# First layer's bank with the router runs three tiles ahead of the other two; turn to the second half interleaved with the left-over products

## The reference, cut to what matters

```
x = x + ffn0(cond0(x))      # cond0: per batch a 64x64 channel mix from an attention over 8 kernels, plus bias
                            # ffn0: x W^T + sum over 8 experts of w * (x A) B, w from a router:
                            #   h = relu(layernorm(x gw1^T + gb1) * gamma + beta); gates = h gw2^T + gb2
                            #   top 2 of 8, softmax; an expert's slot counts only if its total count
                            #   over all 4096 rows is within the capacity of 1536
x = x + ffn1(cond1(x))      # cond1: grouped conv, 9 taps, 4 groups, plus context and bias
                            # ffn1: x W^T + b + experts weighted by softmax(q.k), through A and Bm
```

## Time and profile before

| what | us |
|---|---|
| median of 3 runs (lowest, highest) | 1365.05 (1363.78, 1366.47) |
| the profiled execution | 1364.99 |
| its span | 1363.0 |
| TensorE busy | 1302.4 |
| VectorE busy | 775.0 |
| ScalarE busy | 277.1 |
| GpSimd busy | 247.1 |

### The profile page before, as it was taken

How to read it: one execution, slowest core, us unless ns; L and a number is a source line. 1 busy time by engine, 2 the same in 40 slices (tenths; PEclk the granted TensorE clock), 3 DMA queues, 4 the chain that set the end, 5 groups by cost and what they waited for, 6 DMA issues and landing times.

```text
span 1363.0 us, 21102 instructions
## 1 busy us (share of the span) xinstructions
PE 1302.4 (96%) x7239; PEld 1211.0 (89%) x7239; DVE 775.0 (57%) x1907; ACT 277.1 (20%) x513; POOL 247.1 (18%) x147
## 2 busy tenths in 40 slices
PE   5899999999999994879999999999999999999999
PEld 4899999999999993768998988989889889898897
DVE  2599887777777773555445454454544544545442
ACT  3333222222222221211111111111111111111110
POOL 1244332232232222400100100101001011010010
PEclk8899999999999996789999999999999999999999
DMA  5344333333333327442342433433424334344320
GB/s 212 105 168 153 118 119 122 114 119 121 115 119 119 102 71 188 151 109 68 93 106 66 108 90 82 106 75 96 101 66 111 86 83 105 75 97 100 77 54 31
DMA packets 100364, 143.17 MB, mean 105 GB/s; under 512 B 5104, under 2 KB 76912, under 8 KB 100336
## 3 DMA queue, kind: packets, MB, share of 16 engines
q1 hardware_dynamic: 100336, 142.80, 37.4%
HBM read 89.00 MB, written 53.78 MB: 105 GB/s over the span
## 4 chain that ended last, share of the span: by engine, by line
PE 87%; DVE 7%; DMA 3%; issue 1%; ACT 1%; POOL 0%; SPq 0%; DVEq 0%; ACTq 0%; POOLq 0%
PE ps L980 26%; PE ps L982 26%; PE ps L981 26%; PE ps L1096 6%; PE ps L1097 2%; DVE mix_hl L716 2%; DMA staging<-in_w 1%; DMA x_round<-row 1%; DVE lhs_l L723 1%; DVE weights L706 1%; PE ps L1018 1%; DVE row L737 1%; DMA z<-x_round 1%; DVE part L728 0%; ACT weights L524 0%
## 5 line engine op out<-in xcount | busy, mean ns | idle before, releaser
L980 PE MATMUL ps<-weights,lhs_h 128*128 128x396 f32 (+2 forms) x1792 | 634.9, 354 | 21.0 <-DVE weights L706 19.1
L982 PE MATMUL ps<-weights,lhs_l 128*128 128x396 f32 (+2 forms) x1792 | 625.5, 349 | 0.0
L981 PE MATMUL ps<-weights,lhs_h 128*128 128x396 f32 (+2 forms) x1792 | 624.8, 349 | 0.0
L980 PEld LDWEIGHTS ps<-weights,lhs_h 128*128 128x128 f32 x1792 | 340.4, 190 | 45.6 <-DVE weights L706 11.7
L982 PEld LDWEIGHTS ps<-weights,lhs_l 128*128 128x128 f32 x1792 | 339.3, 189 | 21.1
L981 PEld LDWEIGHTS ps<-weights,lhs_h 128*128 128x128 f32 x1792 | 339.8, 190 | 20.2
L509 POOL TENSOR_TENSOR xo<-row,on_all 128x512 f32<-128x512 f32 x64 | 84.2, 1340 | 679.2 <-DMA out_x<-xo 671.6
L473 POOL TENSOR_TENSOR row<-row,biased 128x1184 f32<-128x1184 f32 x32 | 87.7, 2742 | 297.4 <-DVE count L762 285.8
L1096 PE MATMUL ps<-conv_hl,part 128*128 128x256 f32 x512 | 122.8, 330 | 7.3 <-DVE part L869 7.3
L1097 PE MATMUL ps<-conv_hl,part 128*128 128x128 f32 x512 | 114.6, 224 | 0.0
L537 ACT ACTIVATE part<-ps 128x396 fp32r<-128x396 f32 x96 | 48.1, 503 | 291.7 <-PE ps L982 291.7
(11 more groups left out here) (136 smaller groups left out, 1159.2 us busy)
## 6 DMA issues: line engine op xcount, KB each, us to landing
row<-in_xr SPq DMA_DIRECT2D x32, 592.0 KB, 3.8
spill<-row SPq DMA_DIRECT2D x32, 584.5 KB, 3.1
row<-spill SPq DMA_DIRECT2D x31, 584.5 KB, 5.9
z<-x_round SPq DMA_DIRECT2D x32, 516.0 KB, 3.9
xo<-in_xt SPq DMA_DIRECT2D x32, 512.0 KB, 3.3
x_round<-row SPq DMA_DIRECT2D x64, 256.0 KB, 5.5
out_x<-xo SPq DMA_DIRECT2D x31, 512.0 KB, 2.7
staging<-in_w SPq DMA_DIRECT2D x8, 832.0 KB, 5.0
```

The lines of the kernel that those rows point to most:

```text
L980: pe.matmul(out_ap, lhs[0], rhs[0], start=first, stop=False, skip_group_check=True)
L981: pe.matmul(out_ap, lhs[0], rhs[1], start=False, stop=False, skip_group_check=True)
L982: return pe.matmul(out_ap, lhs[1], rhs[0], start=False, stop=last, skip_group_check=True)
```

## The change

- **Bank 0 ahead.** Bank 0 of `w0` is loaded first, in four pieces of two row blocks; banks 1 and 2 follow in two pieces of four row blocks each (`pieces0`). TensorE makes bank 0 of tiles 0, 1 and 2 and the column sums of banks 0 and 1 first. In the period of tile t it makes main(t, 1), mix(t+2, 0), main(t, 2), mix(t, 1), main(t+3, 0), mix(t, 2); the router of tile t+2 runs in it too. Four tiles' input halves and four mix matrices are held (`XB`), in room of the weights that the first layer leaves free. Semaphores of products, halves, mixes and reads are one for each bank.
- **Rows in two parts.** The part of bank 0 and the part of banks 1 and 2 are loaded, initialised and spilled on their own. The last tile's second part lies in `xo`. The router's choices stay in SBUF (`oh_all`, `dv_all`) and leave the spilled row.
- **Gates for all tiles at once.** One exponential and seven VectorE operations over all 32 tiles replace the six and the exponential of each tile; `gates(t)` is one multiplication.
- **The turn interleaved.** What is left of the first layer after the loop (banks 1 and 2 of the last three tiles, and mixes) is laid between the count, the gates, the first gated product, the split of the second layer's weights, and the first convolution. The last mixes use the banks 4 and 6. `z` of tile 0 has its halves in room of `w0`. `keep_warm` is gone from the turn; 24 matmuls of 128 columns stand ahead of the first product. Row 7 of `w1` goes first, and other chunks are split by GpSimd (`by_pool`).

The diff, cut to its core:

```diff
-        chunks = [(a["w0"][:, j], w0[:, :, j, 0, :], w0[:, :, j, 1, :]) for j in range(J)]
+        pieces0 = [(0, 0, 2), (0, 2, 4), (0, 4, 6), (0, 6, 8), (1, 0, 4), (1, 4, 8), (2, 0, 4), (2, 4, 8)]
+        chunks = [(a["w0"][:, k, lo:hi], w0[:, k, lo:hi, 0, :], w0[:, k, lo:hi, 1, :]) for k, lo, hi in pieces0]
-        by_pool = (3, 6, N_LB0, N_CONV, N_LB1, N1, N1 + 1, N1 + 2, N1 + 4, N1 + 6)
+        by_pool = (N_LB0, N_CONV, N_LB1, N1, N1 + 5, N1 + 7)
...
# SyncE, period of tile t
+                if later(t, 1):
+                    sp.wait_ge(mix_read[2], now)
+                    spill12(t - 1, 1 - u)
+                    sp.wait_ge(spilled12[1 - u], left)
+                load_xr12(t + 1, 1 - u)
+                sp.wait_ge(mix_read[0], ahead)
+                spill0(t + 2, u)
+                if before_end(t, 4):
+                    sp.wait_ge(spilled0[u], left)
+                    sp.wait_ge(counted, ahead)
+                    load_xr0(t + 4, u)
+                if before_end(t, 6):
+                    sp.wait_ge(x_lo, more)
+                    load_xt(t + 6, u)
# SyncE, the turn
+            sp.wait_ge(biased12, TILES)
+            sp.dma_start(b1bc, a["b1"].to_broadcast([P, D])).then_inc(b1_in, 16)
+            x1_store(0, 0)
+            chunk(N1 + 3)
+            z_load(0, 0)
+            chunk(N1 + 4)
+            sp.wait_ge(mix_read[2], TILES - 2)
+            spill12(TILES - 3, 1)
+            sp.wait_ge(spilled12[1], (TILES - 2) // 2 * 16)
+            sp.wait_ge(spilled0[1], TILES // 2 * 16)
             load_row(1, 1)
+            chunk(N1 + 5)
+            sp.wait_ge(mix_read[2], TILES - 1)
+            spill12(TILES - 2, 0)
+            sp.wait_ge(spilled12[0], TILES // 2 * 16)
+            load_row(2, 0)
+            sp.wait_ge(mix_read[2], TILES)
+            spill12(TILES - 1, 1)
             chunk(N1 + 6)
             chunk(N1 + 7)
...
# GpSimd, period
+                if before_end(t, 4):
+                    mix_product(t + 4)
+                row_init12(t + 1, 1 - u, it + u)
+                if before_end(t, 3):
+                    row_init0(t + 3, 1 - u, it + 1 + u)
...
# ScalarE: start, period, turn
             split_hi(4)
+            column_sums(0)
             act.wait_ge(cond_pe, 7)
+            bias0_of(0)
+            split_hi(5)
+            y_high(1, 0)
+            bias0_of(1)
+            x_high(3, 3, 1)
+            root(0)
+            split_hi(6)
+            column_sums(1)
+            split_hi(7)
+            bias0_of(2)
+            column_sums(2)
+            bias12_of(0)
+            root(1)
+            def phase_a(t, b, it):
+                y_high(t + 2, 0)
+                bias12_of(t + 1)
+                y_high(t, 1)
+                root(t + 2)
                 y_high(t, 2)
+                if before_end(t, XB):
+                    x_high(t + XB, b, it + 2)
+                if before_end(t, AHEAD):
+                    bias0_of(t + AHEAD)
+            y_high(TILES - 1, 0)
+            bias12_of(TILES - 2)
+            root(TILES - 1)
+            y_high(TILES - 3, 1)
+            act.wait_ge(counted, TILES)
+            act.activation(gex[:, :], dv_all[:, :], ACT.Exp).then_inc(gexp, 1)
+            split_hi(N1 + 1)
+            y_high(TILES - 2, 1)
+            bias12_of(TILES - 1)
+            tw_high(0)
+            y_high(TILES - 1, 1)
             split_hi(N1 + 2)
             split_hi(N1 + 3)
+            y_high(TILES - 3, 2)
+            y_high(TILES - 2, 2)
             z_high(0)
+            conv_high(0, 0)
+            y_high(TILES - 1, 2)
             split_hi(N1 + 4)
             split_hi(N1 + 5)
...
# VectorE: start, period, turn
+            split_lo(4)
+            split_lo(5)
+            y_low(1, 0)
+            mix_matrix(0, 0)
+            x_low(3, 3)
+            mix_matrix(1, 1)
+            evict(0, 0, 0)
+            route(0, 0)
+            split_lo(6)
+            mix_matrix(2, 2)
+            split_lo(7)
+            evict(1, 1, 0)
+            route(1, 1)
+            def phase_a(t, b, it):
+                if later(t, 1):
+                    evict(t - 1, 1 - u, 2)
+                y_low(t + 2, 0)
+                mix_matrix(t + AHEAD, (b + AHEAD) % XB)
+                y_low(t, 1)
+                evict(t + 2, u, 0)
+                route(t + 2, u)
+                y_low(t, 2)
+                evict(t, u, 1)
+                if before_end(t, XB):
+                    x_low(t + XB, b)
+            y_low(T3, 0)
+            evict(T1 - 1, 0, 2)
+            evict(T3, 1, 0)
+            route(T3, 1)
+            y_low(T1, 1)
...
+            gates(0, 0, 0)
+            y_low(T2, 1)
+            evict(T1, 1, 1)
+            tw_low(0)
+            evict(T2, 0, 1)
+            x1_add(0, 0)
+            y_low(T3, 1)
+            split_lo(N1 + 1)
+            y_low(T1, 2)
+            evict(T3, 1, 1)
+            split_lo(N1 + 2)
+            evict(T1, 1, 2)
+            split_lo(N1 + 3)
+            y_low(T2, 2)
+            z_low(0)
+            evict(T2, 0, 2)
+            gates(1, 1, 0)
+            conv_read_low(0, 0, 0)
+            y_low(T3, 2)
+            evict(T3, 1, 2)
+            split_lo(N1 + 4)
...
# TensorE: start
+            keep_warm(24)
+            main(0, 0, 0, 0, 2)
+            column_sums(0, 0, 2)
+            cond(0)
+            main(0, 0, 0, 2, 4)
+            cond(1)
+            column_sums(0, 2, 4)
+            cond(2)
+            main(1, 1, 0, 0, 4)
+            main(0, 0, 0, 4, 6)
+            column_sums(0, 4, 6)
+            main(0, 0, 0, 6, 8)
+            column_sums(0, 6, 8)
+            main(1, 1, 0, 4, 8)
+            cond(3)
+            main(2, 2, 0, 0, 4)
+            cond(4)
+            main(2, 2, 0, 4, 8)
+            column_sums(1, 0, J)
+            mix(0, 0, 0)
+            def phase_a(t, b, it):
+                main(t, b, 1)
+                if at(t, 0):
+                    mix(1, 1, 0)
+                    column_sums(2, 0, J)
+                mix(t + 2, (b + 2) % XB, 0)
+                main(t, b, 2)
+                mix(t, b, 1)
+                main(t + AHEAD, (b + AHEAD) % XB, 0)
+                mix(t, b, 2)
# TensorE: turn (T1, T2, T3 are tiles 29, 30, 31)
+            main(T1, B1, 1, 0, 4)
+            mix(T3, B3, 0)
+            main(T1, B1, 1, 4, 8)
+            main(T2, B2, 1, 0, 5)
+            pe.wait_ge(counted, TILES)
...
+            main(T2, B2, 1, 5, 8)
+            mix(T1, B1, 1)
+            main(T3, B3, 1, 0, 4)
             tw_turn(0)
+            mix(T2, B2, 1)
+            main(T3, B3, 1, 4, 6)
             lora_first(0)
-            keep_warm(28, lb0_h[:, 0:512])
+            main(T3, B3, 1, 6, 8)
+            main(T1, B1, 2, 0, 4)
+            mix(T3, B3, 1)
+            main(T1, B1, 2, 4, 8)
+            main(T2, B2, 2, 0, 4)
+            mix(T1, B1, 2)
+            main(T2, B2, 2, 4, 8)
+            main(T3, B3, 2, 0, 4)
+            mix(T2, B2, 2)
             conv(0, 0)
             conv(0, 1)
-            keep_warm(12, lb0_h[:, 0:512])
+            main(T3, B3, 2, 4, 8)
```

644 lines of the change are left out of this document (350 added, 294 removed).

## The result

The changed kernel took 1353.49 us (median of 4, 1352.31 to 1358.78) against 1365.76 for the kernel before in the same runs (1363.78 to 1367.43). The ratio over all runs is 0.9918, 95% interval 0.9889 to 0.9948 (the two medians alone give 0.9910), so 11 to 12 us were gained where 20 were forecast. It is faster by more than 0.2% and inside the forecast range (1326 to 1360); the median is also inside the forecast's own band (1335 to 1356). The profiled execution was the slowest of the four, 1358.78 us; that is 13.8 us over the forecast, and a second profile of the same kernel further down (1352.55 us) shows which part of that belongs to this one execution.

The account below looks back on a forecast made before the run. TensorE, busy 1302.4 of 1363.0 us, was taken as the bound. Loop end 485.5 plus turn 66.3 plus half clock 2.5 gave 554.3 against 574.17, 19.9 us earlier: 1345 us, range 1326 to 1360.

Parts of the forecast that it names:

- both holes of the start: First layer's start: TensorE stands 5.6 us for the third bank's column sums and 6.4 us for tile 2's mixing product.
- the long waits of the turn: Between the layers: TensorE stands 4.4 us for tile 29, 4.7 for the convolution, 3.2 for the eighth weight row.
- the untouched 7.4 us wait: Second layer, before the third gated product: ScalarE's queue order is unchanged, so the 7.4 us wait stays.
- The half-clock term: End of the turn: matmuls run at half clock after the last wait, costing 2.5 us.
- The first-layer periods: "0": Steady first layer: VectorE's cycle reaches at most 14.5 us, so the period stays 14.64 us, no change.
- The start: 38.3 us lost: TensorE's loss up to the first whole period: 38.3 us against 36.0 before, so 2.3 us more.
- Z + 66.3: Turn: the second layer's eighth weight row starts 66.3 us after Z, the end of the loop's last mixing product.
- the 1.5 us allowed: Turn: the margin on each landing that went into the forecast's own band, 1335 to 1356 us.
- VectorE-bound first layer: Slower rival: routing with GpSimd's row additions makes VectorE's cycle 15.7 us a period, giving 1376 us; chance 0.07.
- Late transfers: Rival: every transfer of the turn is slow, 4 to 5 us more at three places, giving 1358 us; chance 0.12.

Follow-up runs that it names:

- Moving the additions: Changed kernel with GpSimd's two row additions a period waiting for the count of that period's routing: 1345.94 us, ratio 0.9838.
- without the additions: Changed kernel with GpSimd's two row additions a tile cut to 8 columns each, leaving out most of the mixing bias: 1343.77 us, ratio 0.9826.
- the reordered start: Changed kernel with late weight pieces and low halves ahead of the first routing on VectorE, ScalarE likewise: 1352.07 us; added to all other edits together: 1328.29 us.

## Why the prediction was right, and where it was not

**Right.** The direction, the full second layer, the places of both holes of the start, and the long waits of the turn by place and cause: the low half behind the high half behind weight piece 4 (ScalarE stood 7.68 us for the piece, then copied the bank at 526.45), the first tile's convolution behind tile 1's row (VectorE stood 3.28 us for that row; TensorE's wait ended with the convolution's high half, not its low half), the last piece behind GpSimd, and the untouched 7.4 us wait (7.84 now). The half-clock term, 2.5 us, was also met in the first profile: from the eighth row to the next gated product 15.7 us against 13.2 before, for the same work; in the second it was 15.1.

**The first-layer periods: "0".** This is the step that failed. The prediction put up to 2.7 us of GpSimd's additions into the routing, took the VectorE cycle at 14.5 us at most, found that under 14.64, and booked nothing. The routing did lose 2.0 us a period, and the cycle did stay inside the period: VectorE's busy time did not grow (191.9 us of 250, 194.1 before). Wrong was the test. VectorE needs not only to fit its cycle into the period; its results must be there when the next product on TensorE asks. A routing 2 us longer puts the low half behind it 2 us later. VectorE still stood 1.7 us a period for ScalarE's high halves (29.6 us over 17 periods at L894), and even so most periods lost 0.1 to 0.3 us, and those in which GpSimd had one more operation beside the routing up to 2.0. Measured against the forecast's 14.64 us a period: 7.0 us in the loop of the first profile, 4.1 in the second. Moving the additions took all of it away, 420.6 us from the third tile's first mixing product to the last of the loop, as without the additions (420.3).

**The start: 38.3 us lost.** 40.4 were. The order of the holes was right, and the kernel with moved additions shows 5.75 and 6.35 us for the 5.6 and 6.4 worked out. The term left out was the same one: tile 1's routing taken at its undisturbed length, with GpSimd's three operations falling into it. The section on the periods had named that contention; the section on the start did not apply it.

**The turn: eighth row at Z + 66.3.** It was Z + 70.9 in the first profile, 68.3 in the second. Against the forecast of 0.7, 0.5 to 1.1, 4.4, 4.7, 0.7 and 3.2 us the first profile has 2.23 (count), none (gate), 5.30, 2.59, 2.23 and 6.62, the second 0.64, 1.86, 4.25, 3.54, 1.43 and 3.67. In the second each of these terms is within the 1.5 us allowed; in the first the count and the seventh piece lie just outside, the convolution by 2.1 us the other way and the last piece by 3.4. A wait of 1.15 us at tile 1's gated product, in the second, was not forecast. The total was nearer than its written terms: 46.2 us of work and the listed waits (14.8 at most) make Z + 61.0, and the prediction does not say where the other 5.3 us to Z + 66.3 come from. Without the waits the turn took 51.9 us in the first profile and 51.7 in the second, some 5.6 more than the 46.2 of work at full clock; the granted clock of the turn was 0.88.

**The sum**, for the first profile: 2.1 (start) + 7.0 (loop) + 4.6 (turn) + 0.1 (the rest) = 13.8 us, and 1345 + 13.8 = 1358.8. For the second: 2.1 + 4.1 + 2.0, less 0.5 to 0.6 that the half clock behind the eighth row cost less than forecast, = 7.7, and 1352.7 against 1352.55.

**The rivals.** VectorE-bound first layer (0.07): the right mechanism at the right place, at a fifth of its price. It was drawn as a cycle longer than the period, which decides from 15.3 us on; the loss began below that. A chance and a price for "VectorE fits, but late" was missing, and would have lowered the forecast's gain by 4 to 10 us. Late transfers (0.12, 1358): not what happened. The last piece alone was late by 3 us, in one profile of two, where GpSimd's split ahead of it had taken 5.23 us instead of 3.7.

On the port: by the Trainium skill ("SBUF — State Buffer", section "SBUF: two separate sides") VectorE and GpSimd exclude each other for a whole instruction when VectorE's operation has two SBUF inputs, which is all that the prediction took from it, or runs in what the page calls a 2-port performance mode. The rows agree for L915, L916 and the input's low half, which have two SBUF inputs. Held too were the cast of the indices, which reads one tensor, and L914 and the comparisons, which read one tensor and scalars of a partition; whether they ran in that mode no row here says. Low halves and evictions that read PSUM beside SBUF were not held (567 and 559 to 561 ns with and without the additions).

## What to carry to other kernels

An engine with slack over a period can still be the one that is late: after adding up its cycle, follow the one result that the bounding engine asks for first, and see how far it moves. Where GpSimd and VectorE hold each other up, choose what they meet in: a wait of GpSimd on a count that exists already gave 9.7 us here, with the same work done. And a gain that seems lost in a reordering may only be unpaid: the reordered start gave 1.6 us alone and 4.9 once VectorE's queue had been shortened.

## What was not expected of the hardware

- GpSimd is held by VectorE as VectorE by GpSimd: its addition of 396 columns took 1.03 to 1.05 us in most periods of the changed kernel and 2.04 beside the input's low half, for which VectorE needed 2.05 to 2.11 instead of 1.22.
- The clock of the start differs from execution to execution. In nine profiles of kernels with the same order of work on TensorE up to there, and the same waits, the rise that lasted came between 17 and 26 us, and the first mixing product started at 37.2 us where it came earliest and at 41.0 where it came latest. 24 small matmuls at the very start, ending 1.1 us before the first real one, gained nothing that these runs can tell.
- Executions of one kernel on one chip differ by 7 us (changed kernel again: 1350.71 to 1357.37). Its two profiles differ in the periods and the turn, partly in whom GpSimd's operations meet (its longer addition starts when a row has landed: 85.9 us of its idle time from 200 to 450 us); their starts agree. The kernel before stayed within 4.4 us in eleven runs, though its VectorE was held as long in its periods; why it spreads less is open.
